# Mixture of experts: the scatter adds weighted results into two token tables, and the last stage reads two rows per token

## The reference, cut to what matters

```python
tidx, tw = _gate(x, gate_w, gate_bias)            # 8 experts and 8 weights per token
w_dense = zeros((T, E)).at[arange(T)[:, None], tidx].add(tw)
def body(acc, ws):
    wg, wu, wdn, cw = ws
    hmid = silu(x @ wg) * (x @ wu)
    return (acc + cw[:, None] * (hmid @ wdn), None)
y, _ = scan(body, zeros_like(x), (We_gate, We_up, We_down, w_dense.T))
return y + shared                                  # added to the residual x
```

## Time and profile before

| | |
|---|---|
| time, median of 3 runs | 1046.62 us (1043.81 to 1052.59) |
| profiled execution, its own time | 1047.51 us |
| its span, first to last instruction | 1045.1 us |
| busy share PE / DVE / ACT / POOL | 74% / 45% / 26% / 28% |
| POOL gathers, 92 | 91.9 us busy |
| POOL scatters, 92 | 90.9 us busy |

### The profile page before, as it was taken

How to read it: one execution, slowest core, us unless ns; L and a number is a source line. 1 busy time by engine, 2 the same in 40 slices (tenths; PEclk the granted TensorE clock), 3 DMA queues, 4 the chain that set the end, 5 groups by cost and what they waited for, 6 DMA issues and landing times. The chain is left out here.

```text
span 1045.1 us, 20476 instructions
## 1 busy us (share of the span) xinstructions
PE 777.6 (74%) x6957; PEld 525.3 (50%) x6957; DVE 475.1 (45%) x1360; ACT 270.2 (26%) x562; POOL 291.9 (28%) x321
## 2 busy tenths in 40 slices
PE   4999997668473998986997767764956776676746
PEld 3465565246341454554544656553635555555535
DVE  3232225367363232223364778368965333333325
ACT  2122121454251121211256231022012222222250
POOL 0200000101140200000013344013047777777740
PEclk9999998779786999998799555788989999999987
DMA  9989960200681389990194430010058888888876
GB/s 343 389 322 416 400 266 1 80 2 2 257 319 45 126 338 360 413 392 7 32 196 104 113 84 4 2 41 1 1 164 239 255 248 261 256 254 258 249 249 240
DMA packets 70615, 201.88 MB, mean 193 GB/s; under 512 B 12145, under 2 KB 37457, under 8 KB 64657
## 3 DMA queue, kind: packets, MB, share of 16 engines
q1 hardware_dynamic: 59410, 174.72, 48.7%
q0 software_dynamic: 8832, 24.13, 7.8%
q10 hardware_dynamic: 2304, 2.10, 0.6%
HBM read 185.51 MB, written 15.40 MB: 192 GB/s over the span
## 5 line engine op out<-in xcount | busy, mean ns | idle before, releaser
L1763 POOL DMA_INDIRECT moe_xg<-xn_rows,moe_idx x92 | 91.9, 999 | 75.0 <-DVE moe_idx L1723 49.5
L1697 PE MATMUL ps<-moe_xgT,moe_wgu 128*128 128x128 f32 x736 | 102.7, 283 | 7.4 <-DVE moe_xgT L1728 7.4
L1772 POOL DMA_INDIRECT y_rows<-moe_ysb,moe_row x92 | 90.9, 988 | 29.4 <-issue 25.3
L1697 PEld LDWEIGHTS ps<-moe_xgT,moe_wgu 128*128 128x128 f32 x736 | 91.1, 195 | 10.8 <-DVE moe_xgT L1728 9.3
L1688 PE MATMUL ps<-ident,moe_xg 128*128 128x128 f32 x184 | 40.5, 303 | 72.1 <-DMA moe_xg<-xn_rows,moe_idx 71.8
L1747 ACT ACTIVATE moe_hs<-ps 128x128 f32<-128x128 f32 x92 | 25.5, 277 | 209.3 <-PE ps L1697 209.3
L1688 PEld LDWEIGHTS ps<-ident,moe_xg 128*128 128x128 f32 x184 | 20.0, 144 | 104.5 <-DMA moe_xg<-xn_rows,moe_idx 78.7
L1728 DVE COPY moe_xgT<-ps 128x256 f32<-128x256 f32 x92 | 39.0, 424 | 70.8 <-PE ps L1688 69.0
L1273 POOL TENSOR_TENSOR ss_dec<-ss_dec,ss_cT 128x256 f32<-128x256 f32 x48 | 38.2, 833 | 102.8 <-ACT ss_dec L1238 70.4
L1342 DVE COPY_PREDICATED ss_gm<-w_c_lvl,ps 128x128 f32<-128x128 int32 x160 | 47.8, 300 | 22.5 <-ACT ss_gm L1248 12.6
L1133 PE MATMUL ps<-xnT,w_win 128*128 128x512 f32 x128 | 58.0, 611 | 0.0
(11 more groups left out here) (324 smaller groups left out, 1461.7 us busy)
## 6 DMA issues: line engine op xcount, KB each, us to landing
x0ctxT<-ctx_T SPq DMA_DIRECT2D x8, 3202.0 KB, 19.4
x1ctxT<-ctx_T SPq DMA_DIRECT2D x8, 3202.0 KB, 19.3
x0ctxN<-ctx SPq DMA_DIRECT2D x8, 3072.0 KB
x1ctxN<-ctx SPq DMA_DIRECT2D x8, 3072.0 KB
moe_wgu<-moe_gate_up SPq DMA_DIRECT2D x92, 256.0 KB
moe_wdn<-L_ffn_We_down SPq DMA_DIRECT2D x92, 128.0 KB
moe_yg<-y_rows SPq DMA_DIRECT2D x8, 1024.0 KB, 7.6
ss_dec<-seg_rows SPq DMA_DIRECT2D x8, 768.0 KB, 16.2
```

The source lines that it names most:

```text
L1697: mm = pe.matmul(ps[:, 2 + a2, x * P:(x + 1) * P], wgu[:, a4, h, x, :], xgT[:, a2, h, :], start=h == 0, stop=h == DH - 1)
L1763: nc.gpsimd.indirect_dma_start(out=xg[:, a4, :], out_offset=None, in_=xn_rows, in_offset=bass.IndirectOffsetOnAxis(ap=idx[:, a4:a4 + 1], a ...
L1772: nc.gpsimd.indirect_dma_start(out=y_rows, out_offset=bass.IndirectOffsetOnAxis(ap=row[:, a4:a4 + 1], axis=0), in_=ysb[:, a4, :], in_offse ...
```

## The change

- The token rows in DRAM grow from 256 to 320 numbers: SP also stores the 64 expert weights of each token (`cwt`) beside its row, so the gather brings them along (`xg` is 128 x 320).
- In the loop DVE reads the tile's expert number (four are packed in one integer, `packed`), copies that weight column to `wt`, and ACT's copy of the result becomes a scaled copy. `weight_of` is gone.
- `y_rows` is replaced by `sums`: two tables of 1024 + 128 rows. Tiles with an even number go to the first, odd ones to the second (`pad`, `parity`). Padding slots of a tile go to the 128 spare rows. The scatter now adds (`compute_op=ALU.add`): SP clears both tables with one DMA before. As tiles of one table may hold the same token, the scatter of tile k waits until that of tile k-2 has landed.
- The last stage reads two rows per token (256 KB per token tile, eight buffers, no ring) and DVE adds both to the residual. The diagonals, PE's sums and DVE's multiplications are gone.

```diff
-                    sp.dma_start(xn_rows.rearrange("(j p) d -> p j d", p=P), xn[:]).then_inc(s_rows, 16)
+                    sp.dma_start(xn_rows[:, 0:D].rearrange("(j p) d -> p j d", p=P), xn[:]).then_inc(s_rows, 16)
+                    sp.wait_ge(s_z, 1)
+                    sp.dma_start(sums.rearrange("(x p) d -> p x d", p=P), bc(zero[:], 1, 2 * (NT + 1))).then_inc(s_zero, 16)
+                    sp.wait_ge(s_cwt, 1)
+                    sp.dma_start(xn_rows[:, D:D + E].rearrange("(j p) e -> p j e", p=P), cwt[:]).then_inc(s_rows, 16)
...
+                    nc.vector.memset(zero[:], 0.0).then_inc(s_z, 1)
...
-                    nc.vector.tensor_tensor(cwt[:], cwt[:], bc(tot[:], 2, E), ALU.mult)
+                    nc.vector.tensor_tensor(cwt[:], cwt[:], bc(tot[:], 2, E), ALU.mult).then_inc(s_cwt, 1)
+                    nc.vector.tensor_copy(parity[:], c_iota[:])
+                    nc.vector.memset(etabs[:], 0.0)
+                    for i in range(4):
+                        nc.vector.memset(digit[:, :, i:i + 1], float(E ** i))
+                    dve.drain()
+                    nc.vector.tensor_scalar(parity[:], parity[:], 1, None, ALU.bitwise_and)
+                    dve.drain()
+                    nc.vector.tensor_copy(pad[:], parity[:])
+                    nc.vector.tensor_scalar(spare_row[:], c_col[:], float(T), None, ALU.add)
+                    dve.drain()
...
+                    nc.vector.tensor_copy(etabs[:, 3:3 + P], ps[0:1, 3, 0:P])
+                    dve.drain()
+                    nc.vector.tensor_tensor(digit[:], digit[:], etabs[:].rearrange("o (g i) -> o g i", i=4), ALU.mult)
+                    dve.drain()
+                    nc.vector.tensor_reduce(packf[:], digit[:], AX, ALU.add)
+                    dve.drain()
+                    nc.vector.tensor_copy(packed[:], packf[:])
                     dve.wait_ge(s_im, NT * 8)
-                    nc.vector.tensor_tensor(rowt[:], ps[:, 4, 0:P], c_spare[:], ALU.max)
                     nc.vector.tensor_scalar(idxt[:], ps[:, 4, 0:P], float(-P * P), 0.0, ALU.add, ALU.max)
+                    nc.vector.tensor_scalar(through_row[:], ps[:, 4, 0:P], 0.0, spare_row[:, 0:1], ALU.is_equal, ALU.mult)
                     dve.drain()
                     nc.vector.tensor_scalar(idxt[:], idxt[:], 3, None, ALU.arith_shift_right)
+                    nc.vector.scalar_tensor_tensor(through_row[:], pad[:], float(T + P), through_row[:], ALU.mult, ALU.add)
+                    dve.drain()
+                    nc.vector.tensor_tensor(rowt[:], idxt[:], through_row[:], ALU.add)
...
-                        if isinstance(n, int) and 4 <= n < PEEL:
-                            weight_of(n - 4)
...
+                            expert = (four(g, m) >> (6 * m)) & (E - 1)
+                            nc.vector.tensor_copy(wt[:, a4:a4 + 1], xg[:, a4, ds(expert + D, 1)])
...
-                            nc.scalar.copy(ysb[:, a4, :], ps[:, 4 + a2, 0:D]).then_inc(s_yc, 1)
+                            nc.scalar.activation(ysb[:, a4, :], ps[:, 4 + a2, 0:D], ACT.Copy, scale=wt[:, a4:a4 + 1]).then_inc(s_yc, 1)
...
+                            added = 0 if static and n < 8 else nc.gpsimd.to_reg((round_of(g, m, 8) + 1) * 16)
+                            pool.wait_ge(s_zero, 16)
                             pool.wait_ge(s_yc, ready)
                             pool.wait_ge(s_rw, ready)
-                            nc.gpsimd.indirect_dma_start(out=y_rows, out_offset=bass.IndirectOffsetOnAxis(ap=row[:, a4:a4 + 1], axis=0),
-                                                         in_=ysb[:, a4, :], in_offset=None).then_inc(s_ys[a4], 16)
+                            if not (static and n < 8):
+                                pool.wait_ge(s_ys[m], added)
+                            nc.gpsimd.indirect_dma_start(out=sums, out_offset=bass.IndirectOffsetOnAxis(ap=row[:, a4:a4 + 1], axis=0),
+                                                         in_=ysb[:, a4, :], in_offset=None, compute_op=ALU.add).then_inc(s_ys[a4], 16)
...
+                        sp.dma_start(yg[:, j, :, :], sums.rearrange("(a x p) d -> x p a d", a=2, p=P)[j]).then_inc(s_yg[j], 16)
...
+                        dve.wait_ge(s_yg[j], 16)
+                        nc.vector.tensor_tensor(xt[:, j, :], xt[:, j, :], yg[:, j, 0, :], ALU.add)
+                        dve.drain()
+                        nc.vector.tensor_tensor(xt[:, j, :], xt[:, j, :], yg[:, j, 1, :], ALU.add).then_inc(s_ya, 1)
```

More of the change, by code:

```diff
@@ L56, in perceiver @@
         neghalf = sb("neghalf", [P, 32])
-        xn_rows = nc.dram_tensor("xn_rows", (T, D), F32).ap()
+        xn_rows = nc.dram_tensor("xn_rows", (T, D + E), F32).ap()
         ffn_rows = nc.dram_tensor("ffn_rows_dram", (T, D), F32).ap()
-        y_rows = nc.dram_tensor("y_rows", (P * P + T * 8, D), F32).ap()
+        sums = nc.dram_tensor("expert_sums", (2 * (T + P), D), F32).ap()
         s_x = sem("x_loaded")
@@ L1428, in experts @@
             home = own("home", [P, NT, 8])
-            w8 = own("w8", [P, NT, 8])
-            pick = own("pick", [P, NT, E])
+            w8 = own("w8", [P, NT])
+            zero = own("zero", [P, D])
+            parity = own("parity", [P, P], I32)
+            pad = own("pad", [P, P])
+            through_row = own("through_row", [P, P])
+            spare_row = own("spare_row", [P, 1])
+            etabs = own("etabs", [1, P + 4])
+            packed = own("packed", [1, P // 4 + 1], I32)
+            packf = own("packf", [1, P // 4 + 1])
+            digit = own("digit", [1, P // 4 + 1, 4])
             in_tile = own("in_tile", [P, 4, P])
@@ L1708, in _, with four @@
                 def _(dve):
[L1709 to L1715, removed]
+                    words = {}
+                    def four(g, m):
+                        if m == 0 or not words:
+                            words["now"] = dve.value_load(packed[0:1, ds(g, 1)], min_val=0, max_val=E ** 4 - 1)
+                        return words["now"]
                     def step(n, m, g, live):
-                        if isinstance(n, int) and 4 <= n < PEEL:
-                            weight_of(n - 4)
                         if live(0):
@@ L1784, in _ @@
                     run(sp, step, 0)
-            RING = 4
-            yg = own("yg", [P, RING, 8 * D])
-            s_yg = [sem(f"moe_collected{r}") for r in range(RING)]
+            yg = own("yg", [P, NT, 2, D])
+            s_yg = [sem(f"moe_collected{j}") for j in range(NT)]
             s_ya = sem("moe_result_added")
-            diag = own("diag", [P, NT // 2, 8, P])
-            s_dg = sem("moe_weight_diagonals")
-            s_ws = sem("moe_weighted_sum")
             with nc.Block(no_gpsimd_drain=True) as block:
@@ L1798, in _ @@
                     for j in range(NT):
-                        wait(sp, s_ya, j - RING + 1)
-                        sp.dma_start(yg[:, j % RING, :], y_rows[P * P + j * 8 * P:P * P + (j + 1) * 8 * P, :].rearrange("(p k) d -> p (k d)", k=8)
-                                     ).then_inc(s_yg[j % RING], 16)
-                @block.tensor
-                def _(pe):
-                    for j in range(1, NT, 2):
-                        pe.wait_ge(s_yg[j % RING], 16 * (j // RING + 1))
-                        pe.wait_ge(s_dg, j // 2 + 1)
-                        for k in range(8):
-                            mm = pe.matmul(ps[:, j // 2, 0:D], diag[:, j // 2, k, :], yg[:, j % RING, k * D:(k + 1) * D],
-                                           start=k == 0, stop=k == 7)
-                        mm.then_inc(s_ws, 1)
+                        sp.dma_start(yg[:, j, :, :], sums.rearrange("(a x p) d -> x p a d", a=2, p=P)[j]).then_inc(s_yg[j], 16)
                 @block.scalar
                 def _(act):
-                    for j in range(1, NT, 2):
-                        for k in range(8):
-                            ins = nc.scalar.activation(diag[:, j // 2, k, :], ident[:], ACT.Copy, scale=w8[:, j, k:k + 1])
-                        ins.then_inc(s_dg, 1)
                     for j in range(NT):
```

24 lines of the change are left out of this document (9 added, 15 removed).

## The result

The changed kernel took **1088.5 us** (median of 4 runs, 1086.1 to 1094.7) against 1047.0 for the kernel before, timed beside it (1043.8 to 1052.6): ratio 1.040, interval 1.0355 to 1.0445. The forecast was 1058 us, 1.1% slower; the loss is four times that. The profiled execution took 1086.08 us, its span is 1084.3 against 1045.1.

The account below looks back on a forecast made before the run. POOL's issue of two indirect DMAs, 2.57 us per tile, was taken to bound the loop; +2.3 - 3.8 + 28.5 + 7.0 + 1.1 - 23.2 = +11.9 gave 1058 us. Range 1045 to 1076; 8 in 10, 1027 to 1100.

Parts of the forecast that it names:

- The bound: Tile loop: POOL's issue of two indirect DMAs and their pauses sets the pace, 2.57 us per tile.
- the scatter's instruction: Tile loop, POOL: the adding scatter's instruction was kept at the plain one's 0.99 us.
- last rival: Tile loop: POOL pays for the add, instruction 1.48 us, period 3.18, time 1080; no own chance, slower overall 0.47.
- 85 periods: Tile loop, scatter 0 to scatter 85: 249.0 us against 220.5, +28.5.
- The wait: Tile loop: scatter k starts only after k-2 has landed, making the period 2.93 us; free only if L is under 4.39.
- L: Tile loop: time from an adding scatter's start to its landing, put at 5.1 us, range 4.8 to 5.5.
- r: Tile loop: time from a landing to POOL's next start, put at 0.75 us.
- under 4.22: Tile loop: the plain scatter of tile 4 had landed within 4.22 us, used to bound L from below.
- The engines: Tile loop, DMA queue: the add's second source read raises a scatter's engine time from 0.40 to 0.80 us.
- Routing: Before the tile loop: added small DVE operations and drains cost +2.3 us, bounds 1 to 4.
- First tiles: Gather 0 to scatter 0: without `weight_of` on DVE, 16.4 us become 12.6, -3.8.
- last six: The six scatters after the last gather: each waits for its k-2, 16.0 us instead of 9.04, +7.0.

Follow-up runs that it names:

- e1: Changed kernel with four sum tables instead of two and no wait for the scatter two tiles before: 1088.5 us, ratio 1.037.
- first profile: The kernel before, unchanged, as first profiled, before the change: profiled execution 1047.51 us, span 1045.1 us.
- e2: Changed kernel with a plain store in place of the adding scatter, same tables and wait: 1044.3 us, ratio 0.995.
- e3: Kernel before with only the wait added, each plain scatter waiting for the landing two tiles before: 1067.4 us, ratio 1.021.
- e8: Changed kernel with adding scatters of 128 rows of half the width, 512 bytes instead of 1024: 1082.1 us, one run.
- e5: Changed kernel with all adding scatters into one table, each waiting for the one just before: 1233.4 us, one run.
- first experiments: The variants of the changed kernel and the kernel before run on one chip, where the kernel before took 1049.0 and 1050.6 us.
- e11: Kernel before with a memset of a scratch tile and a drain on POOL behind each plain scatter: 1317.4 us.
- e7: Kernel before with gathered weights and scaled copy, plain scatter, last stage summing eight rows by one strided reduction: 1052.4 us, ratio 1.0015.
- e10: As e7, but the eight rows summed by halving adds on contiguous rows; on another chip, ratio 1.0005 to the kernel before.

## Why the prediction was wrong

**The bound, right.** The loop ran and runs at what POOL can issue; the sum of two instructions and two pauses gives the period to 0.01 us before and after.

**The step that failed: the scatter's instruction.** The forecast kept 0.99 us for it in the sum. It measured 1.586. The text saw this as its last rival, but put it at nothing in the likeliest sum, because gather and scatter cost alike. Both are plain copies, so neither bore on what an add costs. The sign that the text had named for that rival, a scatter instruction far from 0.99 us, is the one that came. That rival's 3.18 us a tile lies near the measured 3.19 (3.22 on average) by luck: its 3.18 was a wait, (5.6 + 0.75) / 2, and POOL alone was to need 3.06, with a price by the row where the measured one is mostly by the instruction. The term "85 periods" was +28.5 and measured +53.6: 85 x 0.60 = 51 is the scatter's instruction, and 274.1 - 271.0 = 3.1 the wait that e1 does not have.

**The wait, near in size and wrong in effect.** L was put at 5.1 and r at 0.75; they measured 4.8 and 0.79. So (L + r) / 2 = 2.80, where the forecast had 2.93. But a period is the larger of the two, 3.19 against 2.80, and the wait cost 5.6 us in the 85 periods and the six last scatters, where the sum had 28.5 and 7.0. That the size is near is in part luck: L is not long mainly because of the add. A plain scatter in the loop takes 4.3 to 4.4 us as well (first profile, e2, e3), so the add is worth about 0.45 of the 4.8. The bound "under 4.22" was the landing of one scatter, and 4.3 is the median.

**The engines.** The forecast had 0.40 us of queue time a transfer become 0.80 for the scatter. Over the same 40 us after:

```profile
q0 software_dynamic: 2421, 3.65, 52.4%
```

and over the 40 us of e2, which leaves out the add alone:

```profile
q0 software_dynamic: 1344, 4.13, 37.9%
```

The packets can be told apart by their bytes. Over the 85 periods a plain scatter in e2 is 32 packets of 4096 bytes, 0.33 us of the 16 engines' time; an adding one in the changed kernel is 128 packets of 1024 bytes, 1.17 us, 3.5 times as much. The Trainium skill (Collectives: The Full Stack, on the bandwidth ceiling) names two source reads where a copy has one; the direction agrees, the factor here is larger. It did not set the time: in e8 the 16 engines carry half the bytes for each scatter and the period stays at 3.19; the loop's DMA share is 0.92 against 0.86, at a slower pace, so with a cheaper instruction the engines may bind next, which no run shows.

**Routing, +7.0 against +2.3**: like with like it is +1.3. At a granted clock of 0.50 in its first microseconds routing takes 74.1 us the old way and 75.4 the new way (the changed kernel twice, e1, e8). The other 5.8 us are the first profile's 68.3, at a clock of 1.00 there; e5, the new way at 1.00, takes 70.2. The text read no clock for that stretch, and no step of it foresaw this.

**First tiles, last six, last landing, last stage**: off by 1.0, 2.3, 0.3 and 0.7 us. Of the 4.7 us on the last six 2.2 are POOL's price of the add, which their forecast had not (e1's 11.2 against 9.0), and 2.5 the wait. The last stage is 16 adds behind the first loads, as described.

**The chances.** Slower had 0.47 and came, on the chip of the first experiments. That another chip would give faster by 2.6% no step foresaw, and no row of the one profile could show it.

## What to carry to other kernels

Where an engine is bound by issuing, price a changed instruction on that engine first, and never by the row of another kind: an accumulating indirect DMA of 128 rows costs GpSimd 1.59 us against 0.99, mostly by the instruction, so narrower rows don't help (e8) and fewer, larger ones should, which was not run. A wait's cost is what stands over the other bound: the same wait cost 13 us at a period of 2.57 and 3 at 3.19. And time a close choice on more than one chip: a kernel that runs at the edge of what one engine can issue may be the one that loses when something else slips in.

## What the runs showed of the hardware

- POOL's instruction for an indirect scatter: plain 0.84 us + 1.2 ns a row, adding 1.29 us + 2.3 ns a row (lines through 64 and 128 rows), the adding one the same for 512 and 1024 bytes a row. The queue's packets follow: 92 steps give 8832 with the plain scatter, 17664 with the adding one, at either width, and 11776 with 64 adding rows.
- A scatter's time on the 16 DMA engines: 0.33 us plain (32 packets of 4096 bytes, e2), 1.17 adding (128 packets of 1024 bytes, changed kernel).
- Landing in the loop, medians from the start of the instruction: 4.3 to 4.4 us plain, 4.8 adding, 3.8 with one adding scatter at a time (e5), 2.37 (plain) and 3.80 (adding) for the last one with nothing beside it. An indirect DMA that waited for a landing starts 0.79 to 0.80 us after it (e3, e5, changed kernel).
- A drain on GpSimd behind a memset waited for the landing of the scatter ahead of it too (e11): the next gather never started sooner than 0.95 us after it.
- A strided reduction of 2048 elements to 256 took 3.58 us on DVE, the same sum by contiguous halving adds 2.34.
- On the chip of the first experiments the kernel before takes 1049 us; on the three others that ran it 1118, 1118 and 1111. There ACT waits up to 6.9 us, about every third tile, for something no row names. Kernels with POOL at 3.04 or 3.19 us a tile lose little or nothing to it, those at 2.57 some 65 us. What it waits for stays open, the more so as these traces hold half or fewer of the updates of the scatters' landings. The clock there is 0.80 to 0.83 against 0.99 in the loop; in the stall shown it falls after the stall. The halving-sum kernel was never timed on the first chip; from e7's 1052 less the 8.6 us by which e10's last stage is shorter, an estimate is 1044 us there.
